# Attention before a mixture of experts: V projected for the eight token tiles, and each unit's overlapping V rows brought together by transfers within SBUF

## The reference

```python
q = (x @ wq.T).reshape(b, t, N_HEADS, HEAD_DIM).transpose(0, 2, 1, 3)
k = (x @ wk.T).reshape(b, t, N_KV_HEADS, HEAD_DIM).transpose(0, 2, 1, 3)
v = (x @ wv.T).reshape(b, t, N_KV_HEADS, HEAD_DIM).transpose(0, 2, 1, 3)
scores = jnp.einsum('bhtd,bhsd->bhts', q, k_full) / np.sqrt(HEAD_DIM)
mask = (k <= q) & ((k < SINK) | (k >= q - WINDOW + 1))     # SINK = 4, WINDOW = 32
attn = _masked_softmax(scores, mask)
out = jnp.einsum('bhts,bhsd->bhtd', attn, v_full)
return out.transpose(0, 2, 1, 3).reshape(b, t, N_HEADS * HEAD_DIM) @ wo.T
```

## Time and profile before

| | |
|---|---|
| median of 3 runs | 529.23 us (528.64 to 529.54) |
| the profiled execution | 529.58 us, span 527.8 us |
| PE busy | 506.1 us (96%), 2939 matmuls |
| DVE, ACT, POOL busy | 410.0, 312.7, 145.7 us |
| V stage on PE | 25.8 to 49.3 us |
| P times V of unit 0, of unit 1 | 57.88, 59.90 us |

### The profile page before, as it was taken

The page is one execution under the profiler, slowest core; times in us unless marked ns, Lnnn a source line. Parts: engine busy times, 40 slices in busy tenths (PEclk is TensorE's granted clock), DMA queues, the critical chain, the costliest instruction groups (busy, mean ns, idle before and its releaser), DMA issues.

```text
span 527.8 us, 9002 instructions
## 1 busy us (share of the span) xinstructions
PE 506.1 (96%) x2939; PEld 427.1 (81%) x2939; DVE 410.0 (78%) x900; ACT 312.7 (59%) x783; POOL 145.7 (28%) x285
## 2 busy tenths in 40 slices
PE   5999999999999999999999999989988999999996
PEld 4778899999999987678888888758877768888884
DVE  5626567667675898899998999965886779899777
ACT  3656878688687754665443445998762355443342
POOL 2241425344243320110110302379434120020110
PEclk9999999999999999999999999999999999999999
DMA  7320100000001303000040000000000000000101
GB/s 281 105 95 1 36 7 2 2 0 2 2 2 25 131 2 140 6 1 0 1 140 1 2 0 1 1 1 2 0 2 0 1 1 1 1 0 1 40 2 40
DMA packets 5789, 14.23 MB, mean 27 GB/s; under 512 B 624, under 2 KB 2928, under 8 KB 5744
## 3 DMA queue, kind: packets, MB, share of 16 engines
q1 hardware_dynamic: 5744, 13.67, 7.4%
HBM read 12.62 MB, written 1.05 MB: 26 GB/s over the span
## 4 chain that ended last, share of the span: by engine, by line
PE 67%; DVE 19%; issue 6%; ACT 5%; POOL 2%; DMA 1%; DVEq 0%; ACTq 0%; POOLq 0%
PE psum L172 55%; PE psum L475 4%; DVE xs L1973 2%; PE psum L507 2%; DVE ln_stats L212 2%; DVE f_t L1296 1%; DVE xn L232 1%; PE psum L240 1%; DVE f_ch L1365 1%; DVE f_ch_hl L1379 1%; DVE xT_hl L254 1%; POOL ln_rstd L226 1%; DVE f_mix L1374 1%; ACT f_sil L1182 1%; PE psum L468 1%
## 5 line engine op out<-in xcount | busy, mean ns | idle before, releaser
L172 PE MATMUL psum<-xT_hl,ffn_w_hl 128*128 128x512 f32 x312 | 77.7, 396 | 0.9 <-ACT f_sil L1182 0.6
L172 PE MATMUL psum<-f_um,ffn_w_hl 128*128 128x512 f32 x288 | 72.9, 399 | 1.1 <-DVE f_t L1296 0.6
L172 PEld LDWEIGHTS psum<-xT_hl,ffn_w_hl 128*128 128x128 f32 x312 | 56.4, 189 | 13.3 <-DVE ffn_w_hl L897 1.4
L172 PEld LDWEIGHTS psum<-f_um,ffn_w_hl 128*128 128x128 f32 x288 | 53.1, 188 | 15.0 <-DVE f_um L1308 1.7
L1182 ACT ACTIVATE f_sil<-psum 128x512 f32<-128x512 f32 (+1 forms) x48 | 28.1, 596 | 48.8 <-PE psum L172 48.8
L1206 ACT ACTIVATE f_ch_hl<-f_ch 128x512 fp32r<-128x512 f32 x48 | 30.4, 632 | 42.2 <-DVE f_ch L1365 40.5
L172 PE MATMUL psum<-xT_hl,wq_hl 128*128 128x512 f32 x192 | 52.0, 407 | 0.6 <-ACT qT L574 0.6
L172 PE MATMUL psum<-wo_hl,oT_hl 128*128 128x256 f32 x384 | 50.8, 281 | 1.0 <-DVE oT_hl L707 0.6
L172 PEld LDWEIGHTS psum<-wo_hl,oT_hl 128*128 128x128 f32 x384 | 47.8, 188 | 3.7 <-DVE oT_hl L707 1.1
L574 ACT ACTIVATE qT<-psum 128x512 f32<-128x512 f32 x32 | 35.3, 1104 | 22.5 <-PE psum L172 22.4
L583 ACT ACTIVATE probs<-probs,small 120x66 f32<-120x66 f32 x120 | 39.8, 338 | 8.2 <-DVE small L684 8.2
(11 more groups left out here) (265 smaller groups left out, 1152.4 us busy)
## 6 DMA issues: line engine op xcount, KB each, us to landing
w_raw<-in_wq SPq DMA_DIRECT2D x4, 512.0 KB, 4.4
w_raw<-in_wo SPq DMA_DIRECT2D x4, 512.0 KB, 3.3
ffn_w_raw<-in_ffn SPq DMA_DIRECT2D x3, 576.0 KB, 4.9
ffn_w_raw_far<-in_ffn SPq DMA_DIRECT2D x3, 576.0 KB, 5.0
ssd_w_raw<-in_ssd SPq DMA_DIRECT2D x3, 512.0 KB, 5.4
x_resid<-in_x SPq DMA_DIRECT2D x2, 512.0 KB, 4.5
out_x<-x_resid SPq DMA_DIRECT2D x4, 256.0 KB, 2.1
w_raw<-in_wk SPq DMA_DIRECT2D x1, 512.0 KB, 6.6
```

Source lines behind the costliest of these rows:

```text
L172: i = e.matmul(dst, lhs(a), rhs(b), start=start and n == 0, stop=stop and n == len(TERMS) - 1, **kw)
```

## The change

V is projected for the eight token tiles of 128, not for the eleven blocks. Tile 0 goes where block 0's V was (its first 4 rows are the sink). Tiles 1 to 7 go to a new buffer `v_rest` in the space where `xg_hl` was, which is also the space of `oT_hl`. The twelve gathering copies of ACT are gone. Twenty-one transfers on SP's queue, issued before the load of wo3, then fill blocks 1 to 10 of `v_hl`: two copy the sink rows to all ten blocks, the rest copy the window's rows from the tile or the two tiles in which they lie. Each waits for the low part of its tile. The pieces, as tile, first row, rows: window 1: (0, 96, 32), (1, 0, 90); 2: (1, 58, 70), (2, 0, 52); 3: (2, 20, 108), (3, 0, 14); 4: (2, 110, 18), (3, 0, 104); 5: (3, 72, 56), (4, 0, 66); 6: (4, 34, 94), (5, 0, 28); 7: (4, 124, 4), (5, 0, 118); 8: (5, 86, 42), (6, 0, 80); 9: (6, 48, 80), (7, 0, 42); 10: (7, 6, 122). A row is 2 KB of the high and 2 KB of the low part. P times V of unit 1 on PE, and ACT's eviction of unit 0 (which writes over `v_rest`), wait for all of them.

```diff
-            xg_hl = at("xg_hl", [P, 2, KB, NJ - 1, NKEY], F32R, A_O)
+            v_rest = at("v_tiles", [P, 2, NT - 1, KV * HD], F32R, A_O)
...
-            FIRST_UNITS = {NJ - 6: 0, NJ - 4: 1, NJ - 2: 2}
-            RECIPS = {NJ - 4: 0, NJ - 2: 1}
-            EXPS = {NJ - 6: (0, (0, 1)), NJ - 5: (0, (2, 3)), NJ - 4: (1, range(NB_Q)), NJ - 2: (2, range(NB_Q))}
+            FIRST_UNITS = {NT - 4: 0, NT - 2: 1}
+            RECIPS = {NT - 2: 0}
+            EXPS = {NT - 4: (0, (0, 1)), NT - 3: (0, (2, 3)), NT - 2: (1, range(NB_Q))}
...
+            def v_tile(t, w):
+
+                return v_hl[:, w, 0, :] if t == 0 else v_rest[:, w, t - 1, :]
+
+            def v_rows(t, r):
+
+                return v_hl[r, :, 0, :] if t == 0 else v_rest[r, :, t - 1, :]
+
+            def window_pieces(j):
+
+                a = Q0[j] - WINDOW
+                t, r = divmod(a, P)
+                n = min(P - r, KWIN)
+                return [(t, r, n, SINK)] + ([(t + 1, 0, KWIN - n, SINK + n)] if n < KWIN else [])
+
+            V_MOVES = 2 + sum(len(window_pieces(j)) for j in range(1, NJ))
+
+            def v_windows(e):
+
+                e.wait_ge(s_vlo, 1)
+                for w in (HI, LO):
+                    e.dma_start(f32(v_hl[0:SINK, w, 1:NJ, :]),
+                                f32(v_hl[0:SINK, w, 0:1, :].broadcast_to([SINK, NJ - 1, KV * HD]))).then_inc(s_vw, 16)
+                for j in range(1, NJ):
+                    for t, r, n, to in window_pieces(j):
+                        e.wait_ge(s_vlo, t + 1)
+                        e.dma_start(f32(v_hl[to:to + n, :, j, :]), f32(v_rows(t, slice(r, r + n)))).then_inc(s_vw, 16)
+
             def sync(e):
                 for n, name in enumerate(loads):
+                    if n == 9:
+                        v_windows(e)
...
-                for j in range(NJ):
-                    if j in FIRST_UNITS:
-                        scores(FIRST_UNITS[j])
-                    if j == 0:
+                for t in range(NT):
+                    if t in FIRST_UNITS:
+                        scores(FIRST_UNITS[t])
+                    if t == 0:
                         e.wait_ge(s_wl, 2)
                         e.wait_ge(s_kev, KV)
-                    if j == 1:
-                        e.wait_ge(s_xg, 2 * KB)
-                    if j >= 2:
-                        e.wait_ge(s_vlo, j - 1)
+                    if t >= 2:
+                        e.wait_ge(s_vlo, t - 1)
                     for k in range(KB):
-                        m = three(e, bank(4 + j % 2)[0:NK[j], :],
-                                  lambda w: xT[:, w, k, 0:P] if j == 0 else xg_hl[:, w, k, j - 1, :],
+                        m = three(e, bank(4 + t % 2), lambda w: xT[:, w, k, t * P:(t + 1) * P],
                                   lambda w: wv_hl[:, w, k, :], k == 0, k == KB - 1)
...
                     e.wait_ge(s_plo, u + 1)
+                    if u == 1:
+                        e.wait_ge(s_vw, 16 * V_MOVES)
                     if u < 2:
-                        e.wait_ge(s_vlo, NJ)
+                        e.wait_ge(s_vlo, NT)
...
-                e.wait_ge(LN["hi"], 2 * KB)
-                for k in range(KB):
-                    gather(e, lambda o, i: e.activation(o, i, ACT.Copy), HI, k).then_inc(s_xg, 1)
-                ln["ready"](e)
-                for k in range(KB):
-                    gather(e, lambda o, i: e.activation(o, i, ACT.Copy), LO, k).then_inc(s_xg, 1)
...
                     if j and Q0[j] < Q0[j - 1] + QN[j - 1]:
                         e.wait_ge(s_olo, u)
+                    if u == 0:
+                        e.wait_ge(s_vw, 16 * V_MOVES)
                     e.activation(out_view(oT_hl[:, HI], j), out_psum(u, j), ACT.Copy).then_inc(s_ohi, 1)
```

More of the change, by code:

```diff
@@ L293, in attention @@
             s_wh, s_wl, s_wk = sem("att_w_hi"), sem("att_w_lo"), sem("att_wk_lo_first")
-            s_pz, s_xg, s_kw = sem("probs_wide_zero"), sem("xg"), sem("k_window")
+            s_pz, s_vw, s_kw = sem("probs_wide_zero"), sem("v_windows_in"), sem("k_window")
             s_k, s_kev, s_v, s_vhi, s_vlo = sem("k_mm"), sem("k_ev"), sem("v_mm"), sem("v_hi"), sem("v_lo")
@@ L353, in weight_free @@
                     if g == 1:
-                        e.wait_ge(s_v, NJ)
+                        e.wait_ge(s_v, NT)
                     if g >= 2:
@@ L401, in out_psum @@
                 return bank(4 + u % 2)[:, 0:GROUP * QN[j]].rearrange("p (q h) -> p h q", h=GROUP)
[L403 to L411, removed]
             def pe(e):
@@ L477, in scores @@
                     m.then_inc(s_s, 1)
-                for j in range(NJ):
-                    if j in FIRST_UNITS:
-                        scores(FIRST_UNITS[j])
-                    if j == 0:
+                for t in range(NT):
+                    if t in FIRST_UNITS:
+                        scores(FIRST_UNITS[t])
+                    if t == 0:
                         e.wait_ge(s_wl, 2)
                         e.wait_ge(s_kev, KV)
-                    if j == 1:
-                        e.wait_ge(s_xg, 2 * KB)
-                    if j >= 2:
-                        e.wait_ge(s_vlo, j - 1)
+                    if t >= 2:
+                        e.wait_ge(s_vlo, t - 1)
                     for k in range(KB):
-                        m = three(e, bank(4 + j % 2)[0:NK[j], :],
-                                  lambda w: xT[:, w, k, 0:P] if j == 0 else xg_hl[:, w, k, j - 1, :],
+                        m = three(e, bank(4 + t % 2), lambda w: xT[:, w, k, t * P:(t + 1) * P],
                                   lambda w: wv_hl[:, w, k, :], k == 0, k == KB - 1)
                     m.then_inc(s_v, 1)
-                    if j < GROUP:
-                        queries(j)
+                    if t < GROUP:
+                        queries(t)
                 def p_transpose(u):
@@ L589, in act @@
                 w_hi(e, 4)
[L590 to L596, removed]
+                for t in range(NT):
+                    e.wait_ge(s_v, t + 1)
+                    e.activation(v_tile(t, HI), bank(4 + t % 2), ACT.Copy).then_inc(s_vhi, 1)
+                    if t < GROUP:
+                        q_evac(t)
+                    if t in EXPS:
+                        exps(*EXPS[t])
                 e.wait_ge(s_par, 16)
@@ L684, in row_max @@
                     e.tensor_reduce(NEGM[0:rows, u % 4, 0:parts], masked, AX.X, ALU.max, negate=True).then_inc(s_max, 1)
[L686 to L693, removed]
+                for t in range(NT):
+                    if t in FIRST_UNITS:
+                        row_max(FIRST_UNITS[t])
+                    e.wait_ge(s_vhi, t + 1)
+                    e.tensor_tensor(v_tile(t, LO), bank(4 + t % 2), f32(v_tile(t, HI)), ALU.subtract).then_inc(s_vlo, 1)
+                    if t in RECIPS:
+                        recip(RECIPS[t])
                 e.wait_ge(s_gwh, 1)
```

## The result

The changed kernel takes 557.53 us (median of 5 runs, 556.36 to 558.23) against 529.23 (528.64 to 529.82) before, a ratio of 1.053 with a 95% interval of 1.0516 to 1.0545: 28.3 us slower. Forecast were 547 in 537 to 560, so the direction and the place were right and the rise was 1.6 times the 17.8 forecast (547 against 529.2). The profiled execution has a span of 556.4 us in 558.23.

The account below looks back on a forecast made before the run. PE's own work was taken as the bound. The profiled 529.58 us plus 15.8 for the later P times V of unit 1 and 1.7 for the clock gave 547.1, 0.35 less for the median: 547, range 537 to 560.

Parts of the forecast that it names:

- What bounds the kernel and what is removed: V stage: PE's own work is the bound; eleven V groups become eight, 3 x 1.4 = 4.2 us off PE.
- The gain of 3.5: Up to unit 1's P times V on PE: 4.2 us removed less 0.7 of new waits, 56.4 instead of 59.90.
- less 0.7 of new waits for ACT: V loop and following steps: query chunks wait somewhat more for their evictions, taking 0.7 us off the 4.2 gained.
- How the rows are cut: Window transfers: equal shares on as many engines up to 16 as divide the rows; 94, 118, 122 on two; chance 0.82.
- The price per engine: Window transfers: 24 GB/s an engine, between 21.9 and 25.8, so 786 KB on the busiest takes 32.8 us.
- When it starts and what runs beside it: Transfers after low part 5: start 42.4, end 75.7, so unit 1's P times V comes 15.8 us later than 59.90.
- What went before is done by about 42: SyncE's queue ahead of window 5's second piece: 41 rows and the sink over twelve microseconds, finished by about 42.
- Start: 41.1 + 0.4 issue + 0.9 lead: Window 5's second piece: low part 5 ready at 41.1, then issue and lead, so moving starts at 42.4.
- The sum's own range: Whole kernel: 541 (25.8 to 27 GB/s, no clock loss) to 553 us (20 GB/s, clock loss 1.7).
- The clock: PE idle from 56.4 to 75.7: the granted clock falls and costs 1.7 us, between 1.0 and twice 1.7.
- The even-split rival: Window transfers use all 16 engines whatever their rows, landing at 50 before PE needs them: 525.7 us; chance 0.10.
- the recorded chances: Whole kernel's outcome: faster 0.11, within 0.2% 0.03, slower 0.86.

Follow-up runs that it names:

- halves: The changed kernel with its 94, 118 and 122 row pieces each cut into two equal halves of prime count: 583.8 us, ratio 1.102 to the kernel before.
- both edits: The changed kernel with three pieces cut at multiples of 16 and the sink rows copied by GpSimd: 528.25 us, ratio 0.9976 to the kernel before.

## Why the prediction was right, and where it was 11 us short

*What bounds the kernel and what is removed.* Right in kind: PE was the bound, 3 groups of 1.4 us went. The gain of 3.5 was twice what it should have been: the run without transfers gained 1.7. The step that failed is "less 0.7 of new waits for ACT"; the new waits are 1.7 us (2.58 against 0.84 before), so PE was ready at 57.8 and not at 56.4. The largest, 1.25, stands where the forecast puts the scores of unit 0 right behind the last of the first four query chunks: ACT must evict that chunk first, and before the change a V group lay between.

*How the rows are cut.* Right, and this decided the sign. Cutting 122 into 112 + 10, three pieces at multiples of 16, and three into primes moved the time by -7.7, -21.0 and +26.3 us, where shares on the busiest engine of 180, 88 and 400 rows instead of 233 stood against it. The rule cited for it (the Trainium skill, "DMA: Bandwidth & Descriptors", the section on the semaphore's 16) agrees with these runs for one and for two engines, and for always the same ones, since otherwise halves would not have cost 26 us. For the counts that it gives 9 to 15 engines no run here shows the number.

*The price per engine.* 24 GB/s forecast, 25 measured where two work alone.

*When it starts and what runs beside it.* This is where 11.1 us were lost (75.7 forecast, 86.83). "What went before is done by about 42" was wrong, and so was "Start: 41.1 + 0.4 issue + 0.9 lead". The 94 rows were issued at about 48.2, over 6 us late, for three reasons. Low part 5 was ready at 43.0 and not at 41.1, by the 1.25 us that PE waits before unit 0's scores and a V stage that began 0.4 later (26.19 against 25.80); this 1.9 is there without the sink too. I priced the sink's rows at nothing: they are 160 KB through four partitions, at 34 and 23 GB/s, and SyncE waits behind them; without them the pair goes 3.6 us earlier and the release is 4.8 earlier. And I priced a transfer's issue at 0.33 us from loads; the piece ahead of the 94 rows took 1.6. From 48.2, the remaining 186 rows at 25 GB/s are 30.5 us, which with lead and end gives 80; the other 6 or 7 us I put down to the stretches in which all engines work and each moves 13 to 16 GB/s instead of 25 (204 at 0.99, 225 at 0.86). That last part is worked out, and where exactly it lies stays open: pieces still queued from before 48.2 may have a share in it, and no run took it apart.

*The range.* The sum's own range, 541 to 553, was missed. The stated one, 537 to 560, holds 557.5 because it was widened for engines that are slower within SBUF. Two engines alone weren't slower (25 GB/s each); the late issue, for which no margin was reckoned, used most of that room. That the range held is in part luck.

*The clock.* 1.7 forecast from the one place in the trace where it fell; 1.5 to 1.6 measured for the changed kernel, by 19.56 us against 18.04, 18.02 and 17.94 at a clock of 1.00. Well sized, and it isn't a constant: the same stretch took 20.06 us with halves and with the sink on GpSimd, 20.26 with one cut and 21.08 with three, so 2.0 to 3.0 us more than 18.04, within the 1.0 to 3.4 that I gave.

*The even-split rival.* I gave it 525.7 with 350 GB/s for sixteen engines. Had it been true, the kernel would probably still have been slower than before: with nearly even shares it took 536.6, since the sink's rows held up SyncE and sixteen engines within SBUF then gave 204 GB/s; with the sink's rows out of the way it took 528.25. So the chance that I gave to faster rested on a rate taken from HBM loads and on the sink's rows costing nothing. (In the recorded chances, the cases named add up to 0.10 for faster and 0.87 for slower; 0.11 and 0.86 stand there.)

## What to carry to other kernels

Before a transfer is put on a path that an engine waits for, factor its row count: here counts of twice a prime (94, 118, 122) ran on two engines and their halves on one, as if the largest divisor up to 16 set the number. Cutting such a count at a multiple of 16 costs one issue more; three cuts gave back 21 of 28 us. A recomputation that costs 4 us of the bounding engine is cheap beside moving the same data: 5.2 MB within SBUF are 25 us of all sixteen engines at the 204 GB/s measured, and PE got only 1.7 us for it at best, 1.3 with both edits. Give the small transfers a price too: two of 80 KB each, through four partitions, held back everything queued behind them. When a stall is shortened rather than removed, look at what PE does in what is left: two microseconds of idling cost 1.5 more by the clock.

## What was not expected of the hardware

- Within SBUF, two engines moved 49 to 50 GB/s and one 25, but sixteen only 204 to 230 at shares of 0.86 to 0.99.
- With transfers between rows of four partitions in the queue, two windows of the trace show 34 and 23 GB/s at shares of 0.26 and 0.23; with these transfers gone the same windows show 241 and 178.
- A transfer's issue on SyncE took 0.33 us for a 128-row load and 0.62 to 9.65 for the eighteen from `v_rest`; the longest stood behind a piece that two engines had yet to move.
- GpSimd copied 4 x 5120 elements in 4.4 us (8.87 for two).
- A stall of 8.2 us on PE was followed by a costlier stretch at the low clock (3.0 us lost) than one of 29.2 us (1.5 lost), in one execution each.
- A gap of 2.1 us on PE, behind others of 1.05 and 0.25 within twelve microseconds, was followed by a granted clock of 0.57 over 3.6 us.
